# Attention on one core: wider transposes of the row maxima, a normalisation moved on ScalarE, four buffers for exponentials, GpSimd's splits in halves

## What is computed

```python
attn = jnp.einsum('bhqd,bhkd->bhqk', q, k) * scale
attn = jnp.where(causal, attn, -jnp.inf)
a = jnp.clip(attn, -100.0, 100.0)
m = jnp.max(a, axis=-1, keepdims=True)
e = jnp.exp(a - m)
p = e / (jnp.sum(e, axis=-1, keepdims=True) + 1e-06)
p = p + 1e-08
p = p / jnp.sum(p, axis=-1, keepdims=True)
out = jnp.einsum('bhqk,bhkd->bhqd', p, v)
```

## Time and profile before

| | us |
|---|---|
| median of 3 runs | 2519.19 (2515.4 to 2524.26) |
| the profiled execution | 2521.44 |
| its span in the trace | 2519.7 |
| causal elements, some 60 to 600 of the span | 540 |
| first plain elements, some 600 to 1120 | 520 |
| second plain elements, some 1720 to 2240 | 520 |

### The profile page before, as it was taken

How to read it: one execution, slowest core, us unless ns; L and a number is a source line. 1 busy time by engine, 2 the same in 40 slices (tenths; PEclk the granted TensorE clock), 3 DMA queues, 4 the chain that set the end, 5 groups by cost and what they waited for, 6 DMA issues and landing times. The chain is left out here.

```text
span 2519.7 us, 45366 instructions
## 1 busy us (share of the span) xinstructions
PE 2351.4 (93%) x14436; PEld 1392.6 (55%) x14436; DVE 1857.4 (74%) x3688; ACT 1402.0 (56%) x2991; POOL 1360.1 (54%) x1420
## 2 busy tenths in 40 slices
PE   5999999999999999989999799888999999989998
PEld 3555555544444444338899577663344444359997
DVE  5999999999778888864333488967788888844333
ACT  3666666665777777763233243225777777653332
POOL 6456656663234555454655499943345555345655
PEclk9999999999999999999999899988999999999999
DMA  5433333333434444425655300025434444244654
GB/s 157 111 103 113 106 102 108 97 109 101 117 109 123 138 137 122 111 87 171 214 190 184 118 1 17 21 78 143 120 103 132 133 133 126 69 148 162 214 183 143
DMA packets 253406, 305.85 MB, mean 121 GB/s; under 512 B 32658, under 2 KB 228337, under 8 KB 253172
## 3 DMA queue, kind: packets, MB, share of 16 engines
q1 hardware_dynamic: 241636, 275.37, 36.5%
q0 software_dynamic: 10176, 26.27, 3.1%
q10 hardware_dynamic: 1360, 1.31, 0.2%
HBM read 210.32 MB, written 92.84 MB: 120 GB/s over the span
## 5 line engine op out<-in xcount | busy, mean ns | idle before, releaser
L705 ACT ACTIVATE prob_af<-sct_af 128x512 f32<-128x512 f32 (+1 forms) x864 | 483.0, 582 | 257.9 <-PE sct_af L513 252.6
L784 DVE TENSOR_REDUCE neg_max_af<-sc_af 128x1 f32<-128x512 f32 (+3 forms) x864 | 548.7, 662 | 86.6 <-PE sc_af L490 81.9
L784 DVE TENSOR_REDUCE neg_max_f<-sc_f 128x1 f32<-128x512 f32 x512 | 333.4, 684 | 75.1 <-PE sc_f L490 72.1
L705 ACT ACTIVATE prob_f<-sct_f 128x512 f32<-128x512 f32 x512 | 289.4, 598 | 134.0 <-PE sct_f L513 131.6
L513 PE MATMUL sct_af<-stack_q_af,stack_k_af 99*128 99x512 bf16 (+3 forms) x1024 | 320.4, 343 | 4.0 <-ACT prob_af L705 3.3
L490 PE MATMUL sc_af<-stack_k_af,stack_q_af 96*128 96x512 bf16 (+3 forms) x1024 | 320.2, 343 | 2.4 <-DVE neg_max_af L784 2.4
L1636 PE MATMUL y_ps_e<-w_r,hT_e 128*128 x1120 | 255.9, 381 | 8.0 <-issue 6.1
L541 PE MATMUL out_af<-prob_af,v_aug_af 128*32 128x512 f32 (+3 forms) x2048 | 234.0, 529 | 21.3 <-DVE prob_af L814 19.4
L814 DVE SCALAR_TENSOR_TENSOR prob_af<-prob_af,w_r 128x512 f32<-128x512 f32 (+2 forms) x224 | 237.6, 1071 | 14.1 <-ACT prob_af L705 12.9
L1823 DVE TENSOR_TENSOR y_e<-y_ps_e,b_e 128x256 f32<-128x256 f32 x70 | 29.7, 424 | 289.2 <-PE y_ps_e L1636 286.4
L1636 PEld LDWEIGHTS y_ps_e<-w_r,hT_e 128*128 128x128 f32 x1120 | 207.2, 190 | 39.2 <-issue 13.6
(11 more groups left out here) (396 smaller groups left out, 4624.8 us busy)
## 6 DMA issues: line engine op xcount, KB each, us to landing
w_r<-in_f_W_dram SPq DMA_DIRECT2D x66, 1024.0 KB, 5.2
stack_k_af<-k_parts_d SPq DMA_DIRECT2D x64, 384.0 KB, 4.2
k_parts_d<-parts_af SPq DMA_DIRECT2D x187, 128.0 KB
q_parts_d<-parts_af SPq DMA_DIRECT2D x96, 128.0 KB
stack_q_af<-q_parts_d SPq DMA_DIRECT2D x64, 192.0 KB, 3.0
stack_k_f<-k_parts_d SPq DMA_DIRECT2D x32, 384.0 KB, 4.3
w_next<-in_f_W_dram SPq DMA_DIRECT2D x12, 1024.0 KB, 5.1
k_parts_d<-parts_f SPq DMA_DIRECT2D x91, 128.0 KB
```

The lines of the kernel that those rows point to most:

```text
L705: nc.scalar.activation(dst, src.rearrange("p (h q) -> p h q", h=len(heads)), ACT.Exp).then_inc(S.exp_done, 1)
L784: nc.vector.tensor_reduce(M.neg_max[:, qt, heads[0]:heads[-1] + 1], src, AX.X, ALU.max, negate=True).then_inc(S.max_done, 1)
```

## The change

It has four parts.

1. The tile of the maxima's parts is 128 columns wide, of which 48 are used and the other 80 are zeroed once per call. PE transposes all 128 columns; ACT still copies 48 rows.
2. In slot 7, `norm_x` stands after i = 1 and no longer after i = 3.
3. Exponentials have four buffers, kt = 0 to 3: two in `prob` and two in the idle banks `w1_0` and `w1_1`. The last element of each call keeps two, and SP waits for the element before it to be through before it loads weights there.
4. In the causal layer each of POOL's three subtractions is issued as two of 128x256.

```diff
+    def four(n):
+        return n != last
+    def prob_no(n, kt):
+        return kt if four(n) else kt % 2
+    def prob_of(n, kt):
+        b = prob_no(n, kt)
+        return M.prob[:, b] if b < 2 else M.more_prob[b - 2]
+    prob_free, prob_user = {}, {}
+    for n in range(first, end):
+        for g in range(NG):
+            for kt in range(KT):
+                prob_free[n, g, kt] = prob_user.get(prob_no(n, kt), 0)
+                prob_user[prob_no(n, kt)] = pv_count(n, g, kt)
...
+            sp.wait_ge(S.pv_done, pv_count(last - 1, NG - 1, KT - 1))
...
-                    last = nc.tensor.transpose(M.gen_bf[bank_of[use]][0:12 * KT, 0:P], M.max_parts[:, :, :, :].rearrange("p a h t -> p (a h t)"),
+                    last = nc.tensor.transpose(M.gen_bf[bank_of[use]][:, 0:P], M.max_all[:, :],
                                                C.ident_bf[:, :])
...
-                if pv_count(n, g, kt) > 2:
-                    act.wait_ge(S.pv_done, pv_count(n, g, kt) - 2)
+                if prob_free[n, g, kt] > 0:
+                    act.wait_ge(S.pv_done, prob_free[n, g, kt])
...
-                    if s in (6, 7) and i == 3:
+                    if (s, i) in ((6, 3), (7, 1)):
                         norm_x(n + 2, (0, 1) if s == 6 else (2, 3))
...
+            nc.vector.memset(M.max_all[:, 12 * KT:P], 0.0)
...
-                nc.gpsimd.tensor_tensor(M.parts[:, j, 1, :], full, top, ALU.subtract).then_inc(S.split_step, 1)
+                pieces = [slice(0, T // 2), slice(T // 2, T)] if causal(n) else [slice(0, T)]
+                for c in pieces:
+                    done = nc.gpsimd.tensor_tensor(M.parts[:, j, 1, c], full[:, c], top[:, c], ALU.subtract)
+                done.then_inc(S.split_step, 1)
...
+    M.max_all = sb("max_parts", [P, P], BF16)
+    M.max_parts = M.max_all[:, 0:12 * KT].rearrange("p (a h t) -> p a h t", a=3, h=4)
```

More of the change, by code:

```diff
@@ L541, in pv @@
                     last = nc.tensor.matmul(bank[32 * i:32 * i + 32, q0:T], M.v_aug[:, kt, 4 * g + i, :],
-                                            M.prob[:, kt % 2, i, 0:T - q0], start=(kt == 0), stop=(kt == 0 if causal(n) else last_kt),
+                                            prob_of(n, kt)[:, i, 0:T - q0], start=(kt == 0), stop=(kt == 0 if causal(n) else last_kt),
                                             skip_group_check=causal(n) and kt > 0)
@@ L698, in exp @@
                 act.wait_ge(S.t_ps, u + 1)
-                if pv_count(n, g, kt) > 2:
-                    act.wait_ge(S.pv_done, pv_count(n, g, kt) - 2)
+                if prob_free[n, g, kt] > 0:
+                    act.wait_ge(S.pv_done, prob_free[n, g, kt])
                 cols = T - kt * P if causal(n) else T
                 src = M.sct[u % 2][:, 0:len(heads) * cols]
-                dst = M.prob[:, kt % 2, heads[0]:heads[-1] + 1, 0:cols]
+                dst = prob_of(n, kt)[:, heads[0]:heads[-1] + 1, 0:cols]
                 nc.scalar.activation(dst, src.rearrange("p (h q) -> p h q", h=len(heads)), ACT.Exp).then_inc(S.exp_done, 1)
@@ L812, in clip @@
                 dve.wait_ge(S.exp_done, u + 1)
-                p = M.prob[:, kt % 2, hs, 0:T - kt * P]
+                p = prob_of(n, kt)[:, hs, 0:T - kt * P]
                 nc.vector.scalar_tensor_tensor(out=p, in0=p, scalar=1.0, in1=M.floor[:, g % 2, hs, kt * P:T],
@@ L1075, in split @@
                 full, top = M.qkf[:, j % 2, :], M.parts[:, j, 0, :]
-                nc.gpsimd.tensor_tensor(M.parts[:, j, 1, :], full, top, ALU.subtract).then_inc(S.split_step, 1)
+                pieces = [slice(0, T // 2), slice(T // 2, T)] if causal(n) else [slice(0, T)]
+                for c in pieces:
+                    done = nc.gpsimd.tensor_tensor(M.parts[:, j, 1, c], full[:, c], top[:, c], ALU.subtract)
+                done.then_inc(S.split_step, 1)
                 pool.wait_ge(S.split_step, st + 1)
-                nc.gpsimd.tensor_tensor(full, full, top, ALU.subtract).then_inc(S.split_step, 1)
+                for c in pieces:
+                    done = nc.gpsimd.tensor_tensor(full[:, c], full[:, c], top[:, c], ALU.subtract)
+                done.then_inc(S.split_step, 1)
                 pool.wait_ge(S.split_step, st + 2)
-                nc.gpsimd.tensor_tensor(M.parts[:, j, 2, :], full, M.parts[:, j, 1, :], ALU.subtract).then_inc(S.split_step, 1)
+                for c in pieces:
+                    done = nc.gpsimd.tensor_tensor(M.parts[:, j, 2, c], full[:, c], M.parts[:, j, 1, c], ALU.subtract)
+                done.then_inc(S.split_step, 1)
             def lay_out_v(n, g):
@@ L1285, in attention_memory @@
     M.max_rest = sb("max_rest", [P, KT, 4])
-    M.max_parts = sb("max_parts", [P, 3, 4, KT], BF16)
+    M.max_all = sb("max_parts", [P, P], BF16)
+    M.max_parts = M.max_all[:, 0:12 * KT].rearrange("p (a h t) -> p a h t", a=3, h=4)
     M.max_sb = sb("max_sb", [12 * KT, 2, P], BF16)
     M.prob = sb("prob", [P, 2, 4, T])
+    M.more_prob = [R.w1[i][:, :, :].rearrange("p c f -> p (c f)").rearrange("p (h t) -> p h t", h=4) for i in range(2)]
     M.o_sb = sb("o_sb", [P, T])
```

## The result

The changed kernel takes 2492.97 us in the median of four runs (2488.79 to 2496.89), the kernel before 2519.57 beside it; the ratio is 0.9894, with a 95% interval of 0.9879 to 0.9909. So it is 1.1% faster, 26.6 us, where 26.2 were forecast and the forecast time was 2493. The total is right, but two of its terms were not, and their errors went opposite ways; the experiments show which.

The account below looks back on a forecast made before the run. PE was taken to bound the plain elements and DVE the causal ones. 11.5 + 1 + 10.7 + 0 + 3 = 26.2 us won gave a median of 2493 us against 2519.2, with an 8-in-10 range of 2478 to 2507.

Parts of the forecast that it names:

- Forecast 0.82 for a plain element: Transposes of the maxima: 0.205 us off each, 56 x 0.205 = 11.5 us in the plain elements.
- the 6.9 forecast: Causal elements, sooner normalisation: PE's waits for ACT and DVE's clip wait both go, 6.9 us won.
- So of 0.87 at most 0.17 is won; I take 0.1: Eight plain elements with router work: PE, 0.87 us sooner, would wait for DVE's held-up maxima; 0.8 us won in all.
- Nothing forecast: Four buffers for the exponentials: costed at nothing, bounds 0 to 1 us won.
- 24 x (1 - 0.79) = 5 won: Causal stretch: of 24 us that clips lose to POOL's splits, halving wins 5.
- 9 x 0.25 = 2 lost: Short operations such as the cast, put at 9 us of loss to splits, wait for every piece: 2 us lost.
- My upper bound of 16: Halved splits in the causal layer: at most half of the 33 us lost to them won, 16.
- halving wins 10: One case of the rival that more comes through: the halved splits win 10 us; that rival's chance 0.17.
- Dearer transposes: Rival: the 0.09 us ahead of the maxima's transpose grows to 0.24, nothing won behind; 2514 us, chance 0.05.
- a slower whole: Rival: halving doubles the collisions, each of 180 POOL pieces holding up a DVE operation; 2528 us, chance 0.03.
- The waits come back elsewhere: Rival, plain elements: PE's gain runs into DVE's split or ACT's later exponentials cost it; 2503 us, chance 0.15.
- More comes through: Rival: collisions fall differently, causal elements give 6.6, or halving wins 10; 6 to 16 us better, some 2481, chance 0.17.

Follow-up runs that it names:

- e1: The kernel before with only the 128-column tile, its zeroing and the wider transpose: 2515.4 us, ratio 0.9966.
- e10: The changed kernel with 112 instead of 128 stationary columns in the transpose of the maxima: 2497.5 us, one run.
- e11: The changed kernel with another width of the maxima's transpose in each element of eight, from 48 to 128 columns: 2501.8 us, one run.
- e8: The changed kernel with POOL's three causal subtractions whole, not halved: 2508.8 us, ratio 0.9945.
- e2: The kernel before with only the second pair of normalisations moved to after i = 1 of slot 7: 2521.2 us, ratio 0.9977.
- e7: The changed kernel with two buffers for the exponentials as before: 2491.8 us, ratio 0.9883.
- e6: The changed kernel with the second pair of normalisations back after i = 3 of slot 7 in elements with router work alone: 2487.9 us, ratio 0.9867.
- e5: The changed kernel, with POOL holding the router's product until DVE has split the maxima of that place: 2482.4 us, ratio 0.9836.

## Why the prediction was right, and where it was not

**Part 1, right.** Forecast 0.82 for a plain element, measured 0.84 alone (e1) and nothing in the causal ones, where I had put 1 us. My reason was right in part: the gap belongs to the transpose's form, not to its amount of work. Whether a load that is not hidden is behind it stays open; the profile gives 0.10 us to the load of 48 columns and to that of 128. The page "TensorE: Matmul & The Clock Gate" of the Trainium skill, which I weighed against this part, says in its section "LDWEIGHTS (loading the stationary operand)" that a load lasts its columns divided by 1.2; by that the wider transposes could only have been slower, and no row shows it. The same page's section "Weight-path perf modes" has a fast load only at 128 columns. Had the gap hung on that, e10 and the wider elements of e11 would have kept it, and they did not. The measurement decides: the step is between 64 and 72 columns.

**Part 2, right where there is no router work, wrong where there is, and not isolated in the causal elements.** The elements without router work gave 0.9 each, 3.6 for 3.0 in all. The causal stretch is 6.8 us shorter in e8 than before (556.4 to 549.6), for the 6.9 forecast, but e8 has parts 1 and 3 as well, and part 2 alone (e2) took 10.8 off. The parts don't add there: alone they give -2.1, 10.8, 7.1 and 13.8 by the traces, together 20.2. So the agreement with 6.9 is in part luck. In the elements with router work the step that failed is "POOL's work at that place follows from earlier statistics of DVE and does not move. So of 0.87 at most 0.17 is won; I take 0.1". The router's product did not move, but the values' layout behind it waits for PE, came earlier with PE, and held a fourth short operation of DVE. The eight elements lost 0.43 each instead of winning 0.1, 4.2 us off.

**Part 3, right.** Nothing forecast, nothing found (e7), for the reason given.

**Part 4, the term mis-sized: 3 forecast, 13.4 to 13.8 in the traces (12.8 and 8.3 by the ratios).** The step was "A clip then waits 0.63 as long each time, but POOL has 1.25 times as much to fit in: 24 x (1 - 0.79) = 5 won ... Short operations wait for every piece: 9 x 0.25 = 2 lost". The first half failed. I let the number of meetings grow with POOL's time; but where two clips stand in a row, POOL's next piece waits for the clip, and one short wait takes the place of two long ones (3.78 to 2.29 at rows 9). From e8 to the changed kernel the clips of elements 1 to 6 take 7.4 us less, some 10 for all eight, where I had 5. And I counted DVE's busy time alone: as much again is idle time of DVE that is gone, for which the sum had no term. Why it goes is not settled; in e8 it stands in the five elements with a stretch at half clock and not in the one without, and the changed kernel has no such stretch there. The loss on short operations, though read from a row of a plain element, where POOL's instructions are not split, was not far off its 2: those of 16 columns take 1 us more in elements 1 to 6. My upper bound of 16 did hold the value, and so did the rival "halving wins 10", which I had given a small share of 0.17.

**The sum.** By the traces: part 1 some 10.7 (the plain stretches of e6 are 14.3 us shorter than before, and 3.6 of that is part 2's), part 2 6.8 + 3.6 - 3.4 = 7.0 (the 6.8 with whatever parts 1 and 3 do in the causal elements), part 4 13.4, together 31.1. The three stretches of the table are 31.0 shorter and the rest of the program 1.6 longer, against my 26.2. The profiled run before lay 1.9 above its median and this one 0.9 below, so the medians give 26.6. Being right to a microsecond was luck: -4.2 in part 2's router elements and -1.8 in part 1 against +10.4 in part 4, and the rest is the spread of the runs.

**The rivals.** Dearer transposes and a slower whole are out. "The waits come back elsewhere" was true in eight elements and "More comes through" in eight others; as wholes neither gave its time.

## What to carry to other kernels

When one engine gets earlier, go through the neighbour's queue for instructions that wait for it: those come earlier too, and may land on a third engine's short operations. An instruction of POOL whose result is wanted late is worth holding back with a semaphore until DVE's short operations that PE waits for are through: one wait gave 10 us here, more than the move that it repaired. Cutting POOL's instructions in two helped DVE where clips stand in a row, but every cut lengthens POOL's queue, so before cutting further look for what stands behind, and move results that others wait for ahead of it.

## What the runs showed of the hardware

- A bf16 transpose with up to 64 stationary columns between products of 128 costs 0.09 us ahead and 0.11 behind; from 72 columns on nothing. Why is open: a change of the array's shape fits, but the profile shows PEld at 0.10 us either way and names no wait.
- A DVE operation of 16 columns that takes 0.19 us took 1.26 beside a POOL instruction of 512 columns, and 0.66 beside one of 256: in the four rows at slot 8 each ends 0.03 to 0.06 us after the POOL instruction beside it. The Trainium skill's page "SBUF — State Buffer", section "Who interferes with whom", says that a DVE instruction with two SBUF inputs contends with a GpSimd one that reads SBUF, and of DVE's 2-port modes, which a cast can enter, that whoever issues first gets the shared pair for the whole instruction; the rows agree.
- A POOL subtraction costs 1.15 us for 512 columns, 0.66 for 256 and some 0.42 for 128 at its least, so cutting once costs 16% and twice 46%.
- PE's granted clock fell to 0.50 (the 1.2 GHz level) for 3.4 us seven times in the causal stretch of the kernel before and never in the changed one's; e5, with the same causal code, and e7, without its buffers, have two each. Before, each fall came 0.2 to 2.1 us after the end of a wait of PE for DVE, 1.0 to 1.6 us long; but a wait of 1.63 us in element 3 was followed by none. What a fall costs differs: from slot 1 to slot 9 the elements of before with one take 37.25 to 39.61 us and the one without 37.98, and in e8 they take 37.15 to 37.36 and the one without 37.05. It seems to depend on whether DVE or PE is behind at that moment; no run separates the two.
